# TensorE fetches 36 chunks in place of 32, in turns of 20 late chunks and six fetched ones, with two pairs of tiles in every fifth slot

## The chip, the cores and the metric

One core of one Trainium2 chip runs the whole kernel. The metric is the device time of one execution in microseconds. The kernel before takes 2099.15 us, the median of three runs (2098.36 to 2101.49).

## The reference, cut to what matters

A graph has 6250 nodes with 64 features each and 200,000 edges, sorted by destination. Five graph layers are mixed. All of them are sums over the edges that end in a node, of features of the edge's source:

```python
seg = lambda v: jax.ops.segment_sum(v, dst, num_segments=n)
xs = x[src]
norm = edge_weights / jnp.sqrt(deg_w[src] * deg_w[dst])
gcn = seg(norm[:, None] * xs) @ Wgcn + bgcn
sage = x @ Wsage_s + seg(xs) / deg_c[:, None] @ Wsage_n + bsage
agg_w = seg(edge_weights[:, None] * xs)
gin = ((1.0 + gin_eps) * x + agg_w) @ Wgin + bgin
gconv = x @ Wgc1 + agg_w @ Wgc2 + bgc
eop = seg(edge_weights[:, None] * relu(xs + edge_attr)) @ Wedge + bedge
out = layernorm(x + einsum('k,knd->nd', weights, stack([gcn, sage, gin, gconv, eop])))
```

The work is in two steps per edge: fetch the row of its source node (`xs`), and add products with it to the row of its destination.

## The kernel before

Edges are cut into 196 chunks of 1024, each of 8 tiles of 128 edges. As the edges are sorted, a chunk's destinations lie in a window of 40 nodes. For a chunk, VectorE builds "hots" (for each edge a row of 40 zeros and one entry: 1, the weight, the weight times the root of the degree), adds the edge's attributes to the fetched features, and ScalarE takes the ReLU. TensorE multiplies the features with the hots, tile by tile, into a PSUM bank (`segment_sums`, L1272), and VectorE adds the 40 columns to the sums in SBUF (`add_sums`, L1076). The node rows are fetched in one of three ways:

- *Early* chunks (EARLY = 16): GpSimd gathers raw rows of x before the degrees are known.
- *Late* chunks (148): GpSimd issues eight indirect DMAs per chunk (L572) from a table in DRAM into a ring of UNROLL = 4 chunks. It may write a place of the ring again when TensorE's product of the chunk four before is done (`chunk_product`).
- *Fetched* or *picked* chunks (PICKED = 32): TensorE does the fetch. A chunk is two *units* of HALF = 4 tiles; a unit is two *pairs* of tiles. The node number of an edge is split into a key (node // 7, one of up to 128 partitions where the table lies) and a digit. SP loads the chunk's keys to all partitions (`load_keys`). ScalarE turns them into one-hot matrices for a pair, seven Squares (L696) and one Relu (L699), into one half of `node_hot` (`hot_nodes`). TensorE multiplies each tile's seven one-hots with the high and the low part of the node table in SBUF, 14 matmuls of 462 columns (`pick_tile`, L1293), into one of two PSUM banks. VectorE masks out the digit (L999) and sums (L1003) (`pick`), and after the second pair of a unit does the unit's hots and features (`unit_features`). ScalarE takes the unit's ReLU (`relu_unit`, L687), TensorE its product, 8 matmuls (`unit_product`), VectorE adds it (`add_unit`).

A loop of 4 early steps does the 16 early chunks with the first 16 late ones. Then 16 turns (ROUNDS) follow, the first written out, the other 15 a loop on each of TensorE, ScalarE, VectorE and SP. A turn has 8 *slots* m: each does one late chunk and one pair, so that four slots make one fetched chunk and a turn two. The four last late chunks are the plain step (PLAIN = 1). After that come the output products. GpSimd's gathers are written out for all late chunks. The order on every engine is written by hand as these loops give it, and semaphores with counts hold them together; an engine does nothing ahead of its order.

On TensorE a slot is: late product, two tiles of picks, and in every second slot the product of a unit. On ScalarE: one-hots of the pair, ReLU of the late chunk, and in every second slot the ReLU of a unit. On VectorE: features of the late chunk (waits for its gathers), add of the chunk four before, weights on the hots, then the picks of the pair that TensorE did in the slot before. On SP every second slot issues the attributes of two late chunks (512 KB), each followed by the attributes of a half chunk (128 KB), and once per fetched chunk the keys (256 KB).

The functions that the diff touches, as they are before:

## Time and profile before

| | |
|---|---|
| median of three runs | 2099.15 us |
| profiled execution | 2085.72 us, span 2083.9 us |
| granted TensorE clock, mean | 0.858 |
| TensorE matmul / weight load | 1441.4 us (69%) / 1266.5 us (61%) |
| VectorE / ScalarE / GpSimd | 51% / 44% / 61% |
| late gathers | 1184, 1146.5 us busy |
| matmuls of picks | 3584, 1445.5 us, overlapping |
| DMA | 125.65 MB, mean 60 GB/s |

The profile is one execution. PE is TensorE's matmuls, PEld its weight loads, which run beside them, DVE VectorE, ACT ScalarE, POOL GpSimd, SP the queue that issues most DMAs. A matmul's shown length overlaps with the next one's, so the distance from start to start is what it costs. A group's row has its line, engine, operation, tiles, shapes and count, then the busy time and mean of one, then the idle time of the engine before it and who ended it; "issue" is idle time that nobody's work ended, "remote" a release that the profile can't name. Clock 1.00 is 2.4 GHz.

### The profile page before, as it was taken

To read this page: it belongs to the slowest core of one execution; us is meant where nothing else is said; L and a number is where in the kernel's file an instruction comes from. 1 tells how busy PE (TensorE), PEld (TensorE's weight loads), DVE (VectorE), ACT (ScalarE), POOL (GpSimd) and SP (SyncE) were. 2 spreads that over 40 slices of the span, in tenths; PEclk is the share of its full clock that TensorE was granted. 3 is DMA by queue.
4 is the path that set the end of the run, shared out by engine and by line. 5 is a ranking of instruction groups with operands and counts; after the bars stand their busy time and mean duration, and the time that the engine had idled before them with its cause. 6 is when DMAs were issued, how large, how long until landed. Compare 5 with 4: busy or idle time off the path is not lost.

```text
span 2083.9 us, 26839 instructions
## 1 busy us (share of the span) xinstructions
PE 1441.4 (69%) x7381; PEld 1266.5 (61%) x7381; DVE 1053.7 (51%) x2851; ACT 907.1 (44%) x1515; POOL 1273.2 (61%) x1330
## 2 busy tenths in 40 slices
PE   2000565566877777787877877778788788877876
PEld 1000565565766666676766766667667667756766
DVE  6846274663544445544544544444544454444447
ACT  3847132324544444444544544444544444434433
POOL 6664646665666666666666666666666665666660
PEclk9999986767888888888988888878988988888978
DMA  5111143322222222222222222222222222222214
GB/s 100 24 24 29 43 129 99 103 83 69 53 55 55 53 53 54 61 64 54 54 53 67 53 54 54 54 53 53 56 65 59 54 54 52 67 55 53 55 45 95
DMA packets 86857, 125.65 MB, mean 60 GB/s; under 512 B 28796, under 2 KB 38763, under 8 KB 85463
## 3 DMA queue, kind: packets, MB, share of 16 engines
q0 software_dynamic: 41984, 45.50, 12.8%
q1 hardware_dynamic: 43109, 78.08, 11.8%
q10 hardware_dynamic: 1650, 1.04, 0.3%
q14 instruction: 101, 0.83, 0.1%
q8 instruction: 13, 0.21, 0.0%
HBM read 121.09 MB, written 3.42 MB: 60 GB/s over the span
## 4 chain that ended last, share of the span: by engine, by line
PE 36%; another core or an unknown queue 20%; issue 20%; DVE 11%; ACT 10%; DVEq 2%; DMA 0%; ACTq 0%
PE psum L1293 22%; PE psum L1272 11%; ACT ring L614 4%; ACT node_hot L696 3%; DVE early L1003 2%; DVE ring L1087 2%; DVE sums L1076 2%; PE psum L1325 1%; DVE early L999 1%; ACT ring L662 1%; DVE early L1020 1%; PE psum L1354 1%; PE psum L1355 1%; DVEq L1076 0%
## 5 line engine op out<-in xcount | busy, mean ns | idle before, releaser
L572 POOL DMA_INDIRECT ring<-node_table,e_src x1184 | 1146.5, 968 | 694.7 <-issue 327.2
L1293 PE MATMUL psum<-table_hi,node_hot 128*128 128x462 f32 x1792 | 730.8, 408 | 71.0 <-issue 44.6
L1293 PE MATMUL psum<-table_lo,node_hot 128*128 128x462 f32 x1792 | 714.8, 399 | 40.2 <-issue 39.7
L1272 PE MATMUL psum<-ring 128*128 128x120 f32 x2368 | 371.6, 301 | 228.3 <-issue 180.0
L999 DVE TENSOR_TENSOR early<-psum,digit_hot 128x455 f32<-128x455 f32 x256 | 157.9, 629 | 696.4 <-remote 518.6
L1272 PEld LDWEIGHTS psum<-ring 128*128 128x128 f32 x2368 | 331.7, 212 | 259.5 <-issue 239.3
L696 ACT ACTIVATE node_hot<-early,minus_ids 128x256 fp32r<-128x256 f16 x896 | 370.6, 494 | 239.2 <-remote 205.6
L1293 PEld LDWEIGHTS psum<-table_hi,node_hot 128*128 128x128 f32 x1792 | 370.3, 207 | 146.8 <-issue 71.8
L1293 PEld LDWEIGHTS psum<-table_lo,node_hot 128*128 128x128 f32 x1792 | 369.7, 206 | 97.0 <-issue 55.5
L687 ACT ACTIVATE early<-early 128x256 f32<-128x256 f32 x64 | 26.8, 418 | 600.3 <-DVE early L1020 462.7
L699 ACT ACTIVATE node_hot<-node_hot,ones 128x1792 fp32r<-128x1792 f32 x128 | 229.5, 1793 | 4.2
L1272 PE MATMUL psum<-early 128*128 128x120 f32 x768 | 125.6, 320 | 65.2 <-ACT early L682 46.5
L1076 DVE TENSOR_TENSOR sums<-sums,psum 64x40 f32 (+1 forms) x684 | 134.9, 197 | 56.6 <-remote 21.3
L1272 PEld LDWEIGHTS psum<-early 128*128 128x128 f32 x768 | 120.6, 233 | 70.1 <-ACT early L682 53.7
L538 POOL DMA_INDIRECT early_x<-in_x,early_idx x128 | 122.0, 953 | 65.1 <-issue 47.9
L1003 DVE TENSOR_REDUCE early<-early 128x65 f32<-128x455 f32 x256 | 147.4, 618 | 0.0
L1087 DVE TENSOR_TENSOR ring<-ring,psum 128x320 f32<-128x320 f32 x296 | 131.1, 484 | 4.6
L662 ACT ACTIVATE ring<-attr 128x512 f32<-128x512 f32 x148 | 91.3, 617 | 87.7 <-issue 45.0
L881 DVE SCALAR_TENSOR_TENSOR early<-attr,scratch,psum 128x1024 bf16<-128x1024 f32 x80 | 98.6, 1276 | 37.4 <-issue 37.0
L614 ACT ACTIVATE ring<-attr,scratch 128x1024 bf16<-128x1024 f32 x82 | 93.3, 1138 | 35.0 <-issue 34.1
L1247 PE MATMUL psum<-ring 128*128 128x98 f32 (+1 forms) x8 | 2.0, 435 | 153.1 <-DVE ring L898 153.1
L964 DVE TENSOR_TENSOR attr<-attr,ring 128x512 f32<-128x512 f32 x148 | 101.4, 685 | 0.0
(160 smaller groups left out, 748.2 us busy)
## 6 DMA issues: line engine op xcount, KB each, us to landing
attr<-in_edge_attr SPq DMA_DIRECT2D x73, 512.0 KB
ring<-node_table,e_src POOLq DMA_INDIRECT x1184
src_all<-in_src SPq DMA_DIRECT2D x8, 1024.0 KB
early<-key_rows SPq DMA_DIRECT2D x32, 256.0 KB
early<-in_edge_attr SPq DMA_DIRECT2D x64, 128.0 KB
early<-in_edge_attr SPq DMA_DIRECT2D x16, 256.0 KB
early_x<-degree_rows SPq DMA_DIRECT2D x2, 1568.0 KB, 14.7
early_x<-in_x,early_idx POOLq DMA_INDIRECT x128
```

Source lines behind the costliest of these rows:

```text
L538: nc.gpsimd.indirect_dma_start(out=early_x[:, c, j], out_offset=None, in_=x, in_offset=bass.IndirectOffsetOnAxis(ap=early_idx[:, c, j:j + ...
L572: nc.gpsimd.indirect_dma_start(out=feat[:, u, j, D:BLOCK], out_offset=None, in_=table, in_offset=bass.IndirectOffsetOnAxis(ap=e_src[:, c + ...
L614: last = nc.scalar.activation(signs[0:rows, k % TURNS], row_dst[0:rows, g], ACT.Sign, bias=cuts[0:rows, n:n + 1], scale=-1.0, accum_out=si ...
L662: nc.scalar.activation(feat[:, u, :, 0:D], attr[:, u], ACT.Relu).then_inc(relu_ready, 1)
L696: last = nc.scalar.activation(to[:, :, a], keys_of[k][:, tile:tile + 2], ACT.Square, bias=minus_ids[:, a:a + 1])
L699: nc.scalar.activation(to, to.bitcast(F32), ACT.Relu, bias=ones[:, 0:1], scale=-2.0).then_inc(node_hot_made, 1)
L999: nc.vector.tensor_tensor(out=picks[:, k % 2], in0=pick_ps[k % 2].rearrange("p (b c) -> p c b", b=SPLIT)[:, 0:D + 1], in1=hot_c, op=ALU.mu ...
L1003: last = nc.vector.tensor_reduce(out=feat_g[:, half, k, D:2 * D + 1], in_=picks[:, k % 2], axis=AX.X, op=ALU.add)
L1076: last = nc.vector.tensor_tensor(out=sums[of, k, to], in0=sums[of, k, to], in1=acc[ps, part * WINDOW:(part + 1) * WINDOW], op=ALU.add)
L1087: return nc.vector.tensor_tensor(out=to[:, :, k], in0=to[:, :, 0], in1=by.unsqueeze(2).to_broadcast([P, n, WINDOW]), op=ALU.mult)
L1272: last = nc.tensor.matmul(to[:, 0:3 * WINDOW], features[:, j, 0:2 * D], hots[:, j].rearrange("p k n -> p (k n)"), start=(j == 0), stop=(j ...
L1293: last = nc.tensor.matmul(pick_ps[k % 2], node_hot[:, k, a], part[:, a * SPLIT:(a + 1) * SPLIT].rearrange("p b c -> p (b c)"), start=a == ...
```

## The change

PICKED goes from 32 to 36, so 144 chunks are late. A turn has SLOTS = 20 slots and TURN_CHUNKS = 6 fetched chunks, 24 pairs; there are 6 turns, of which the first is written out, and PLAIN = 2 steps of four chunks at the end. `slot_of` puts pair g into a slot: slots 4, 9, 14 and 19 get two pairs, the others one. `TAKEN` has VectorE take each pair one place later in the order than it is made; `FEATURED` says in which slot a unit's features and ReLU come; the unit's product on TensorE is in the slot after it, now ahead of the slot's picks. Keys stay in two buffers (KEYS = 2).

```diff
-PICKED = 32
+PICKED = 36
-SLOTS = 4
+SLOTS = 20
-TURN_CHUNKS = 2
-TURN_STEPS = TURN_CHUNKS * SLOTS // UNROLL
+TURN_CHUNKS = 6
+TURN_STEPS = SLOTS // UNROLL
+TURN_UNITS = 2 * TURN_CHUNKS
+PAIRS = 2 * TURN_UNITS
+KEYS = 2
-PLAIN = 1
+PLAIN = 2
...
+        def slot_of(g):
+            return g // 6 * 5 + min(g % 6, 4)
+        FETCHED = [[g for g in range(PAIRS) if slot_of(g) == m] for m in range(SLOTS)]
+        TAKEN = [[(g - 1) % PAIRS for g in FETCHED[m][:1]] + FETCHED[m][:-1] for m in range(SLOTS)]
+        FEATURED = {u: slot_of(2 * u + 1) + 1 for u in range(-2, TURN_UNITS)}
+        def unit_at(m, later=0):
+            return next((u for u in FEATURED if FEATURED[u] + later == m), None)
+        def units_added(m):
+            return sum(FEATURED[u] + 1 < m for u in FEATURED) - 2
...
@@ SP, turn
+                    for m in range(SLOTS):
                         if m % 2:
                             load_attributes(EARLY_STEPS + s * TURN_STEPS + m // UNROLL, m % UNROLL // 2)
+                        for k in range(TURN_CHUNKS):
+                            if m == slot_of(4 * k - 5) + 5:
+                                load_keys(s * TURN_CHUNKS + k, k, begun or k >= KEYS)
+                        for u in range(-2, TURN_UNITS - 2):
+                            if m == FEATURED[u] + 5:
+                                load_unit(s * TURN_CHUNKS + (u + 2) // 2, u % 2)
+                        if m in (0, 2) and begun:
+                            load_unit(s * TURN_CHUNKS - 1, m // 2)
...
@@ ScalarE, turn
-                        hot_nodes(s, 2 * c + r // 2, m // SLOTS, r // 2, r % 2)
-                        late_chunk(EARLY_STEPS + s * TURN_STEPS + m // UNROLL, m % UNROLL)
+                        for g in FETCHED[m]:
+                            hot_nodes(s, s * TURN_UNITS + g // 2, g // 4, g // 2 % 2, g % 2)
+                            if g == FETCHED[m][0]:
+                                late_chunk(EARLY_STEPS + s * TURN_STEPS + m // UNROLL, m % UNROLL)
+                        u = unit_at(m)
+                        if u is not None and (begun or u >= 0):
+                            relu_unit(s * TURN_UNITS + u, u % 2)
...
@@ VectorE, turn: features, add and weigh_hots of the late chunk stay
-                        if r in (1, 3) and (begun or m > SLOTS):
-                            dve.wait_ge(added_g, v * UNITS + 2 * c + (r == 3))
+                        elif (begun or m > 2) and (m == 0 or units_added(m) != units_added(m - 1)):
+                            dve.wait_ge(added_g, v * UNITS + s * TURN_UNITS + units_added(m) + 1)
+                        for g in TAKEN[m]:
+                            if m == 0:
+                                if begun:
+                                    take(s * TURN_UNITS - 1, s * TURN_CHUNKS - 1, g)
+                            else:
+                                take(s * TURN_UNITS + g // 2, s * TURN_CHUNKS + g // 4, g)
+                        n = unit_at(m, 1)
+                        if n is not None and (begun or n >= 0):
+                            add_unit(s * TURN_UNITS + n, s * TURN_CHUNKS + n // 2, i * UNROLL + u - LAG + 1)
+                def take(n, c, g):
+                    half, pair = g // 2 % 2, g % 2
+                    pick(n, c, half, (2 * pair, 2 * pair + 1))
+                    if pair:
+                        unit_features(n, c, half)
...
@@ TensorE, turn
-                        late_chunk(i, u)
-                        for pair in range(2):
-                            pick_tile(2 * c + r // 2, 2 * (r % 2) + pair)
-                        if r == 3:
-                            unit_product(2 * c, 0)
-                        if r == 1 and (begun or m > SLOTS):
-                            unit_product(2 * c - 1, 1)
+                        late_chunk(EARLY_STEPS + s * TURN_STEPS + m // UNROLL, m % UNROLL)
+                        u = unit_at(m, 1)
+                        if u is not None and (begun or u >= 0):
+                            unit_product(s * TURN_UNITS + u, u % 2)
+                        for g in FETCHED[m]:
+                            for k in range(2):
+                                pick_tile(s * TURN_UNITS + g // 2, 2 * (g % 2) + k)
```

## Rows read from the trace of the kernel before

**Rows 1.** The page's first part: busy time, share of the span, instructions, by engine
```profile
PE 1441.4 (69%) x7381; PEld 1266.5 (61%) x7381; DVE 1053.7 (51%) x2851; ACT 907.1 (44%) x1515; POOL 1273.2 (61%) x1330
```

**Rows 2.** One line's instructions, L662: 484 to 2027 us, and 499.5 to 656.9 us
```profile
L662 ACT ACTIVATE ring<-attr x129: 609/613/637, 484.1 to 2026.4; 128x512 f32<-128x512 f32 x129
...
L662 ACT ACTIVATE ring<-attr x14: 610/612/616, 499.7 to 656.5; 128x512 f32<-128x512 f32 x14
```

**Rows 3.** Busy time by stretch, turns and end: busy us (instructions) by engine, clock, DMA
```profile
core 0: us, PE busy (x) PEld busy (x) DVE busy (x) ACT busy (x) POOL busy (x), PEclk, DMA share, GB/s
484.00:2026.00 1542.00, 1220.58 (x6106) 1057.52 (x6107) 731.42 (x2114) 681.73 (x1208) 981.09 (x1018) 0.85 0.24 56
2026.00:2084.00 58.00, 40.78 (x299) 39.15 (x298) 41.26 (x94) 20.69 (x26) 5.80 (x7) 0.88 0.38 88
```

**Rows 4.** Timelines of GpSimd and ScalarE from 1990 us on: start, length, instruction
```profile
2023.94 0.94 POOL L572 DMA_INDIRECT ring<-node_table,e_src  x1 [3.33 <-remote]
...
2032.69 0.94 POOL L572 DMA_INDIRECT ring<-node_table,e_src  x1 [0.30 <-issue]
...
2010.29 0.61 ACT L662 ACTIVATE ring<-attr 128x512 f32<-128x512 f32 x1
...
2047.74 0.63 ACT L662 ACTIVATE ring<-attr 128x512 f32<-128x512 f32 x1 [5.80 <-DVE attr L964]
```

**Rows 5.** Groups of instructions by line, GpSimd, 484 to 2026 us
```profile
L572 POOL DMA_INDIRECT ring<-node_table,e_src x1018 | 981.2, 964 | 567.0 <-issue 281.5 <-remote 190.6 <-PE psum L1272 94.9
```

**Rows 6.** Timeline of TensorE, a slot in a clear stretch
```profile
528.98 1.05 PE L1272 MATMUL psum<-early 128*128 128x120 f32 x8
529.86 1.95 PE L1272 MATMUL psum<-ring 128*128 128x120 f32 x16
531.58 0.46 PE L1293 MATMUL psum<-table_hi,node_hot 128*128 128x462 f32 x1
...
537.57 0.93 PE L1272 MATMUL psum<-ring 128*128 128x120 f32 x7
```

**Rows 7.** Busy time by stretch: first and last stall, and a clear stretch
```profile
512.80:524.00 11.20, 6.17 (x12) 3.06 (x13) 0.63 (x1) 0.00 (x0) 6.60 (x7) 0.68 0.25 67
2011.60:2023.70 12.10, 3.70 (x14) 2.86 (x13) 0.68 (x2) 0.00 (x0) 6.87 (x8) 0.65 0.27 66
888.00:910.00 22.00, 21.63 (x132) 19.83 (x130) 12.14 (x34) 10.74 (x19) 15.19 (x16) 1.00 0.23 57
```

**Rows 8.** Timeline of TensorE, a stall and the matmuls after it
```profile
1008.29 0.37 PE L1293 MATMUL psum<-table_hi,node_hot 128*128 128x462 f32 x1
...
1012.86 0.55 PE L1293 MATMUL psum<-table_hi,node_hot 128*128 128x462 f32 x1 [0.19 <-issue]
1015.00 0.55 PE L1293 MATMUL psum<-table_lo,node_hot 128*128 128x462 f32 x1 [1.59 <-issue]
1016.38 0.55 PE L1293 MATMUL psum<-table_hi,node_hot 128*128 128x462 f32 x1 [0.84 <-issue]
...
1019.92 0.59 PE L1293 MATMUL psum<-table_lo,node_hot 128*128 128x462 f32 x1
1020.30 0.59 PE L1293 MATMUL psum<-table_hi,node_hot 128*128 128x462 f32 x1
```

**Rows 9.** Who waited for whom on TensorE, 484 to 2026, then 275 to 450 us
```profile
PE psum L1272 <- issue: 177.9, 198, 3.4
...
PE psum L1293 <- issue: 84.3, 113, 2.6
...
PE psum L1272 <- ACT ring L662: 39.7, 22, 10.0
...
PE psum L1293 <- DVE early L999: 25.2, 15, 3.4
...
PE psum L1272 <- issue: 10.6, 4, 3.2
```

**Rows 10.** DMA queues, 430 to 650 us, then 650 to 2040 us
```profile
q8 instruction: 8, 0.13, 0.2%
...
q14 instruction: 80, 0.66, 0.1%
```

More of the change, by code:

```diff
@@ L216, in build @@
         key_all = key_all.bitcast(F16)
-        keys_of = [key_all[:, k * CHUNK:(k + 1) * CHUNK].rearrange("p (j e) -> p j e", e=P) for k in range(TURN_CHUNKS)]
+        keys_of = [key_all[:, k * CHUNK:(k + 1) * CHUNK].rearrange("p (j e) -> p j e", e=P) for k in range(KEYS)]
         picks = picks.rearrange("p (s c b) -> p s c b", s=2, b=SPLIT)[:, :, 0:D + 1]
@@ L317, in build @@
         key_ready, key_stored = sem("key_ready"), sem("key_stored")
-        key_loaded = [sem(f"key_loaded{k}") for k in range(TURN_CHUNKS)]
+        key_loaded = [sem(f"key_loaded{k}") for k in range(KEYS)]
         key_bias_set, key_row_step = sem("key_bias_set"), sem("key_row_step")
@@ L473, in turn @@
                 def turn(s, begun=True):
-                    for m in range(TURN_CHUNKS * SLOTS):
-                        k, r = m // SLOTS, m % SLOTS
-                        c = s * TURN_CHUNKS + k
+                    for m in range(SLOTS):
                         if m % 2:
                             load_attributes(EARLY_STEPS + s * TURN_STEPS + m // UNROLL, m % UNROLL // 2)
-                        if r == 1:
-                            if begun or k:
-                                load_unit(c - 1, 1)
-                            else:
-                                sp.wait_ge(early_product, (v + 1) * EARLY + 1)
-                            load_keys(c, k, begun)
-                        if r == 3:
-                            load_unit(c, 0)
+                        if m == 1 and not begun:
+                            sp.wait_ge(early_product, (v + 1) * EARLY + 1)
+                        for k in range(TURN_CHUNKS):
[6 more added lines that the diff above has]
+                            load_unit(s * TURN_CHUNKS - 1, m // 2)
                 turn(0, begun=False)
@@ L701, in turn @@
                 def turn(s, begun=True):
-                    for m in range(TURN_CHUNKS * SLOTS):
-                        c, r = s * TURN_CHUNKS + m // SLOTS, m % SLOTS
-                        hot_nodes(s, 2 * c + r // 2, m // SLOTS, r // 2, r % 2)
-                        late_chunk(EARLY_STEPS + s * TURN_STEPS + m // UNROLL, m % UNROLL)
-                        if r == 0 and (begun or m):
-                            relu_unit(2 * c - 1, 1)
-                        if r == 2:
-                            relu_unit(2 * c, 0)
+                    for m in range(SLOTS):
+                        for g in FETCHED[m]:
[5 more added lines that the diff above has]
+                            relu_unit(s * TURN_UNITS + u, u % 2)
                 far_sources(0, 0, 0)
@@ L1032, in turn @@
                 def turn(s, begun=True):
-                    for m in range(TURN_CHUNKS * SLOTS):
+                    for m in range(SLOTS):
                         i, u = EARLY_STEPS + s * TURN_STEPS + m // UNROLL, m % UNROLL
-                        c, r = s * TURN_CHUNKS + m // SLOTS, m % SLOTS
                         if u == 0:
@@ L1046, in turn @@
                             add_early(EARLY - 1, EARLY - LAG + 1)
-                        if r:
-                            half, pair = (r - 1) // 2, (r - 1) % 2
-                            pick(2 * c + half, c, half, (2 * pair, 2 * pair + 1))
-                            if r == 2:
-                                unit_features(2 * c, c, 0)
-                        elif begun or m:
-                            pick(2 * c - 1, c - 1, 1, (2, 3))
-                            unit_features(2 * c - 1, c - 1, 1)
-                            add_unit(2 * c - 2, c - 1, i * UNROLL + u - LAG + 1)
-                        if r == 2 and (begun or m > SLOTS):
-                            add_unit(2 * c - 1, c - 1, i * UNROLL + u - LAG + 1)
+                        for g in TAKEN[m]:
[12 more added lines that the diff above has]
+                        unit_features(n, c, half)
                 def add(c, turn, first):
@@ L1134, in _ @@
                         features(i, u, last=i == LATE_STEPS - 1)
-                        if slot in (1, 3):
-                            dve.wait_ge(added_g, v * UNITS + UNITS + (slot == 3))
+                        if slot < 3:
+                            dve.wait_ge(added_g, v * UNITS + UNITS + slot - 1)
                         add(i * UNROLL + u - LAG, u - LAG, firsts[u])
@@ L1142, in _ @@
                             add_unit(UNITS - 2, PICKED - 1, i * UNROLL + u - LAG + 1)
-                        if slot == 2:
+                        if slot == 1:
                             add_unit(UNITS - 1, PICKED - 1, i * UNROLL + u - LAG + 1)
@@ L1343, in _ @@
                         late_chunk(i, u)
[L1344 to L1345 removed]
+                        if i == LATE_STEPS - PLAIN and u < 2:
+                            unit_product(UNITS - 2 + u, u)
             for g in range(GROUPS):
```

32 lines of the change are left out of this document (15 added, 17 removed).

## The prediction

> **What bounds the kernel now.** I read the page's first part, then the starts of one repeated instruction, busy time by stretch, what GpSimd does at the end, TensorE's timeline in a clear slot and in a bad one, and its waits.
>
> The page's shares give no bound: TensorE 69%, GpSimd 61%, nobody full [rows 1]. The stretch that the change touches has 128 slots, each with one late chunk and one pair of picked tiles. The ReLU of a late chunk (L662) marks a slot: the first of the stretch starts at 484.1 us, the one 128 later at 2026.4 [rows 2], so 1542.3 us, or 12.05 us a slot. That is 74% of the span, and in it TensorE is busy 1220.6 of 1542 us at a mean clock of 0.85, GpSimd 981.1 [rows 3].
>
> Two engines could set 12.05 us. GpSimd issues eight gathers per late chunk; seven steps from 2023.94 to 2032.69 make 1.25 us for each [rows 4], so 10.0 us a slot, and it waits the other 2.05: 190.6 + 94.9 us over the stretch for others [rows 5]. TensorE in a slot at full clock: the 16 matmuls of the late chunk take 1.72 us (529.86 to 531.58), the 28 of two picked tiles 5.99 (531.58 to 537.57, 0.21 each), the 8 of a half unit, due every second slot, 0.88 [rows 6]. Sum: 1.72 + 5.99 + 0.44 = 8.15 us. Over 128 slots that is 1043 us; the other 499 us, 3.90 a slot, TensorE does not work, or works at less than full clock. Most of it is one pattern. In some 34 places of the stretch TensorE all but stops for about 12 us: 12 and 14 matmuls in the first and the last of them, where a clear stretch does 132 in 22 us [rows 7]. Within one, neighbours of the same accumulation start 2.1 and 1.4 us apart with no other engine to release them ("issue"), and after it a matmul of the same shape takes 0.59 us in place of 0.37 and starts every 0.38 in place of 0.21, which is the 1.2 and no more the 2.4 GHz level [rows 8]. Of waits for other engines TensorE shows little: 39.7 us for the ReLU, 25.2 for VectorE's pick (L999), against 177.9 and 84.3 of "issue" [rows 9]. So 65 of the 499 us are waits that other work could fill, and 434 are stalls and slow clock. TensorE bounds the slot, and GpSimd is second with 2 us of slack.
>
> By the Trainium skill (Perfetto Trace Analysis, Identifying the Most-Contended Engine) matmul busy time is no measure for TensorE, and weight-load busy time is to be read: here 1057.5 of 1542 us, 69% [rows 3]. That would leave room on TensorE and is the case of rival C; the releasers of its gaps speak against it.
>
> **The change part by part.**
> (1) Late chunks go from 148 to 144. The 16 of the early stage stay, so 128 + 4 become 120 slots + 8 plain chunks.
> (2) A slot now carries 1.2 pairs (24 in 20) and 0.6 half units (12 in 20): 1.72 + 1.2 x 5.99 + 0.6 x 0.88 = 9.44 us at full clock, +1.29. GpSimd's 10.0 us a slot stands. ScalarE is busy 681.7 us of the 1542, 5.3 a slot, VectorE 731.4, 5.7 a slot [rows 3]; with 1.2 times that each stays below 7 us and hides behind TensorE's 9.4. That cover is gone only if TensorE's slot fell below 7.
> (3) The 3.90 us of lost time. If the stalls come per slot, per late chunk or per microsecond, they stay. The waits in it (65 / 128 = 0.5 a slot) can be filled by the added picks: lower end 3.4. I take 3.7, nearer the upper end, since the chain pick, features, ReLU, next one-hots still runs once per half unit. Slot: 9.44 + 3.7 = 13.14 (12.8 to 13.35). 120 of them: 1577 us (1541 to 1602). Against 1542: +35 (0 to +60).
> (4) The plain end. Before, from the last slot's ReLU at 2010.3 to the last at 2047.7, 37 us pass with four plain chunks [rows 4]. There now are eight, TensorE has no picks there, and the gathers go on at 10.0 us a chunk: +40 if GpSimd has no lead. The ring holds four chunks, and with more slack GpSimd fills it: part of the 40 is prepaid. Lower end +20, I take +32.
> (5) Loop ends. Six rounds of 20 slots in place of 16 of 8, ten fewer on every engine. TensorE's waits name none, so 0; if each had cost its longest "issue" gap, 3.4 us [rows 9], -34.
> (6) The size of TensorE's loop: 8 slots are 8 x 32 + 8 x 56 + 4 x 16 = 768 weight loads and matmuls, 20 slots 640 + 24 x 56 + 12 x 16 = 2176. Queue 8 moves 8 instruction packets, 0.13 MB or 16 KB each, from 430 to 650 us, and has no row from 650 to 2040 [rows 10]: I read it as TensorE's code, resident from then on. While it moved, slots were no slower: 13 of them from 499.7 to 656.5 us, 12.06 each [rows 2]. So fetching ahead costs 0; a jump back to code that has gone costs between 0 and one stall of 12 us [rows 7], at five loop ends: 0 to +60. I take +6, nearest to the 0 of straight code.
> The Trainium skill (Runtime: NRT & Kernel Launch, Instruction fetch mechanics) has TensorE's instruction memory at 2048 instructions in blocks of 256, and a taken branch out of it must fetch first. By that rule the new loop no longer fits, and the sum would be at the upper end of (6); the trace agrees with the block size, and shows no such branch.
> (7) Before the loops, 36 in place of 32 keys and digits: under 1 us. Four more key loads and eight more half-unit loads on SP's queue replace two of the attribute loads. SP issues in order behind waits for ReLUs, two slots ahead as before. VectorE's wait for added_g moves by a slot; behind it are queued its own adds and picks, for which TensorE waits, but what it waits for is its own add of an earlier slot: 0.
> (8) Two pairs in every fifth slot. The second pair's one-hots use the other half of the buffer and cost ScalarE some 4.5 us (5.3 less the ReLUs) against TensorE's 5.99, so 0. If the order added a wait, one 3.4 us gap in each of 24 such slots, +82; I take 0.
>
> Sum: +35 + 32 + 6 = +73 us. On the profiled execution (2085.7 us around a span of 2083.9) that is 2159. The median of the runs is 2099.15, 13 above it; on it **2172 us**.
>
> **Rivals.**
> *B, stalls follow the picks.* From 275 to 450 us, with no picks, TensorE's "issue" before L1272 is 10.6 us in all [rows 9], and afterwards there are 34 stalls for 32 picked chunks. If the picks make them, they cost 434 x 36/32 = 488 us in place of 434 x 120/128 = 407: +81 on the forecast, 2253. Against: in the trace they keep no fixed place in a turn.
> *C, GpSimd's pace decides, and the added picks fall into time that TensorE loses now.* Then a late chunk costs 12.05 us as today, and four fewer save 48: 2051 us. Place: the slot; price: -12.05 per chunk removed; it brings a gain as long as a slot stays below (1542 - 32) / 120 = 12.6 us, for which the lost time has to fall from 3.90 to under 3.1. For it: GpSimd's waits are many and short (190.6 us, [rows 5]), and longer runs of matmuls keep the clock up. Against: filling every wait for others reaches only 3.4.
> *D, the stalls belong to the turn.* Two per round: 12 in place of 32, each worth 434 / 34 = 12.8 us: 256 less, 2172 - 256 = 1916; GpSimd's 1200 us for 120 slots allow it. Against: the first, unrolled turn has them as well (512.8 us, [rows 7]).
> *E, the loop thrashes.* Each of nine blocks in five rounds stalls TensorE by 12 us less the 2 of work in it: +450, 2622. Against: see (6).
>
> **How the numbers follow.** Forecast 0.43, B 0.19, C 0.20, D 0.07, E 0.04, and 0.07 for effects that cancel to within 20 us of the old time, of which 0.02 faster, 0.03 the same, 0.02 slower. About 0.2%, 4 us, is what a measurement of this kernel can tell from no change. Faster: 0.20 + 0.07 + 0.02 = 0.29; same 0.03; slower 0.68. The forecast's own range, by the ends of (3) to (6), is 2099 + 20 - 34 = 2085 to 2099 + 160 = 2259; with the 82 of (8) on top it would be 2341, which I leave out. The range takes in C and B and leaves out D and E: 2045 to 2262.
>
> **What would show it.** (2) and (3): the first and the last slot's L662, 120 apart, 1541 to 1602 us from each other, and GpSimd waiting 3 us a slot. B: more than 36 stretches of 12 us with a dozen matmuls; D: a dozen; C: a slot below 12.6 us. (4): 57 to 77 us between the last slot's ReLU and the last one. (6): a row for queue 8 through the whole stretch, and a gap on TensorE every 20 slots. The forecast is wrong if a slot stays below 12.6 us.

## The result, and the profile after

The changed kernel takes **2125.14 us** (median of four, 2121.18 to 2129.47), the one before, run beside it, 2098.86 (2098.36 to 2101.49): ratio **1.0121**, 95% interval 1.0097 to 1.0145. In a later session (after_again, chip 6) it was 1.0053 (1.0022 to 1.0084). The change makes the kernel slower, by 26 us and not by the 73 that I forecast. The profiled execution went from 2085.7 to 2121.2 us, its span from 2083.9 to 2119.4.

The page's first part (busy time, share, instructions) answers to [rows 1]:
```profile
PE 1499.5 (71%) x7829; PEld 1332.6 (63%) x7829; DVE 1090.4 (51%) x2954; ACT 984.1 (46%) x1647; POOL 1242.1 (59%) x1298
```
L684 is the late chunk's ReLU now. The first row below lists its starts from the first slot to the first plain chunk, 120 later, the second those up to the last; they answer to [rows 2, 4]:
```profile
L684 ACT ACTIVATE ring<-attr x121: 607/613/636, 487.7 to 2028.2; 128x512 f32<-128x512 f32 x121
...
L684 ACT ACTIVATE ring<-attr x128: 607/613/636, 487.7 to 2080.0; 128x512 f32<-128x512 f32 x128
```
With them the 35.5 us of the span split without remainder:

| stretch | before | after | difference | forecast |
|---|---|---|---|---|
| start to the first slot's ReLU | 484.1 | 487.7 | +3.6 | 0 |
| slots, to the first plain ReLU | 1542.3 (128) | 1540.5 (120) | -1.8 | +35, loops +6 |
| first plain ReLU to the last | 21.3 (4 chunks) | 51.8 (8) | +30.5 | +32 |
| last ReLU to the end | 36.2 | 39.4 | +3.2 | 0 |

All of the miss is in the second line: a slot takes 12.84 us, where the forecast had 13.14. TensorE's work in it is 9.44 us at full clock, so 3.40 are lost, against 3.90 before. The 120 slots' 1540.5 us lie just under the 1541 to 1602 that were to show the forecast true. The last of the 120 intervals alone took 27.0 us (before 16.1); without it a slot is 12.72 us.

Busy time of the slots and of the end (columns as in [rows 3]), GpSimd's group (as [rows 5]), TensorE's waits (as [rows 9]; L1298 is the late chunk or half unit, L1319 the pick), and the queues from 650 us on (as [rows 10]):
```profile
487.00:2028.00 1541.00, 1260.54 (x6498) 1105.94 (x6499) 758.45 (x2184) 757.88 (x1336) 922.48 (x960) 0.90 0.23 55
2028.00:2119.00 91.00, 56.44 (x355) 54.19 (x354) 51.33 (x127) 23.27 (x30) 30.81 (x32) 0.76 0.34 78
```
```profile
L594 POOL DMA_INDIRECT ring<-node_table,e_src x960 | 922.5, 961 | 629.0 <-issue 261.3 <-PE psum L1298 194.7 <-remote 173.0
```
```profile
PE psum L1298 <- issue: 143.7, 117, 5.4
...
PE psum L1298 <- ACT ring L684: 66.9, 34, 20.4
PE psum L1319 <- issue: 40.8, 58, 6.9
...
PE psum L1298 <- DVE ring L1113: 24.6, 12, 4.0
...
PE psum L1319 <- DVE early L1021: 13.6, 14, 1.9
```
```profile
q8 instruction: 56, 0.92, 0.3%
q14 instruction: 56, 0.46, 0.1%
```
The reader is to see two movements. TensorE's "issue" time fell from 262.2 to 184.5 us, and the waits for others that these rows show rose from 64.9 to 105.1. Counted in the trace, the stalls of 12 us in the slots went from 34 (414 us) to 16 (205 us), and other pauses of over 0.6 us from 50 (72 us) to 98 (177 us). A stall is a dense run of such pauses, 8 us long or more. With the line drawn a little differently before still has 34 and the kernel after 16 to 19, and in its later session the same kernel had 24: part of the fall to 16 is chance. GpSimd's waits for TensorE and "remote" grew from 285.5 to 367.7 us.

What the stalls hang on shows when GpSimd's timeline is laid beside TensorE's. First GpSimd, kernel after, from 1404 us (the lines left out are gathers 1.25 us apart with 0.30 of "issue"), then TensorE, then that window and a clear one by busy time:
```profile
1409.62 0.95 POOL L594 DMA_INDIRECT ring<-node_table,e_src  x1 [2.69 <-remote]
...
1418.38 0.95 POOL L594 DMA_INDIRECT ring<-node_table,e_src  x1 [0.30 <-issue]
1419.63 0.95 POOL L594 DMA_INDIRECT ring<-node_table,e_src  x1 [0.31 <-issue]
...
1428.39 0.95 POOL L594 DMA_INDIRECT ring<-node_table,e_src  x1 [0.30 <-issue]
1434.52 0.95 POOL L594 DMA_INDIRECT ring<-node_table,e_src  x1 [5.18 <-PE psum L1298]
```
```profile
1418.86 0.38 PE L1319 MATMUL psum<-table_lo,node_hot 128*128 128x462 f32 x1
1421.95 0.93 PE L1298 MATMUL psum<-ring 128*128 128x120 f32 x6 [2.71 <-ACT ring L684]
1423.21 0.26 PE L1298 MATMUL psum<-ring 128*128 128x120 f32 x1 [0.33 <-issue]
1425.31 0.36 PE L1298 MATMUL psum<-ring 128*128 128x120 f32 x1 [1.84 <-issue]
1428.11 0.36 PE L1298 MATMUL psum<-ring 128*128 128x120 f32 x1 [2.44 <-issue]
1430.21 0.36 PE L1298 MATMUL psum<-ring 128*128 128x120 f32 x1 [1.74 <-issue]
1431.61 0.36 PE L1298 MATMUL psum<-ring 128*128 128x120 f32 x1 [1.04 <-issue]
1432.32 1.41 PE L1298 MATMUL psum<-ring 128*128 128x120 f32 x5 [0.35 <-issue]
```
```profile
1418.90:1432.30 13.40, 2.96 (x13) 2.01 (x11) 2.89 (x10) 0.63 (x1) 8.00 (x9) 0.67 0.15 25
1440.00:1462.00 22.00, 21.16 (x122) 18.98 (x122) 13.47 (x38) 12.92 (x25) 11.33 (x12) 1.00 0.23 57
```
Eight gathers are one chunk. At 1409.62 GpSimd begins a chunk after a pause, at 1419.63 the next one with none. From that moment matmuls of one accumulation start 1.4 to 2.8 us apart, until 3 us after the sixteenth gather ends. Going back to the kernel before with this in hand: 34 of 128 chunks there begin less than 1.5 us after the end of the gather before them ("no pause" from here on), and the 34 stalls begin each within -1.0 to +2.7 us of one of these. The stall of [rows 8] is one; GpSimd in the kernel before:
```profile
996.47 0.94 POOL L572 DMA_INDIRECT ring<-node_table,e_src  x1 [2.56 <-remote]
...
1006.67 0.94 POOL L572 DMA_INDIRECT ring<-node_table,e_src  x1 [0.31 <-issue]
...
1020.13 0.94 POOL L572 DMA_INDIRECT ring<-node_table,e_src  x1 [3.79 <-remote]
```
In the kernel after there are 19 such chunks and 16 stalls, all at one of them. What lets GpSimd go on is an early product of TensorE, the one that frees its place in the ring. Laid side by side in the trace of before (124 chunks): where it was done 5 us or more ahead of the end of the last gather, 28 of 41 chunks began with no pause, at 3 to 5 us 5 of 19, and later than that none of 64. I had read GpSimd by its sum and its waits, and never against the stalls.

### The profile page after: what moved, and what is told of

It is laid out like the page before. It is cut to its first block, busy times and chain, and to the rows that moved or that the text cites. A ratio compares the mean times of both kernels' runs of the same rounds, so it can differ in the third digit from the quotient of the medians.

```text
span 2119.4 us, 27847 instructions
## 1 busy us (share of the span) xinstructions
PE 1499.5 (71%) x7829; PEld 1332.6 (63%) x7829; DVE 1090.4 (51%) x2954; ACT 984.1 (46%) x1647; POOL 1242.1 (59%) x1298
## 4 chain that ended last, share of the span: by engine, by line
PE 36%; issue 27%; another core or an unknown queue 17%; DVE 9%; ACT 7%; DVEq 2%; SPq 1%; POOL 1%; DMA 0%; ACTq 0%; POOLq 0%
PE psum L1319 21%; PE psum L1298 12%; ACT node_hot L718 5%; PE psum L1349 1%; DVE early L1021 1%; DVE sums L1102 1%; DVE early L1025 1%; DVE ring L1113 1%; ACT ring L684 1%; DVE attr L986 1%; POOL ring L594 1%; PE psum L1378 1%; PE psum L1379 1%; DVEq L1102 0%
## 5 line engine op out<-in xcount | busy, mean ns | idle before, releaser
L594 POOL DMA_INDIRECT ring<-node_table,e_src x1152 | 1115.0, 968 | 770.2 <-issue 314.9
L1319 PE MATMUL psum<-table_hi,node_hot 128*128 128x462 f32 x2016 | 788.8, 391 | 39.7 <-issue 24.9
L1319 PE MATMUL psum<-table_lo,node_hot 128*128 128x462 f32 x2016 | 773.3, 384 | 16.5 <-issue 15.8
L718 ACT ACTIVATE node_hot<-early,minus_ids 128x256 fp32r<-128x256 f16 x1008 | 417.4, 495 | 460.1 <-remote 325.0
L1298 PE MATMUL psum<-ring 128*128 128x120 f32 x2304 | 362.5, 312 | 265.0 <-issue 140.8
L1298 PEld LDWEIGHTS psum<-ring 128*128 128x128 f32 x2304 | 334.6, 223 | 301.9 <-issue 230.1
L1021 DVE TENSOR_TENSOR early<-psum,digit_hot 128x455 f32<-128x455 f32 x288 | 177.2, 629 | 591.2 <-remote 422.1
L1319 PEld LDWEIGHTS psum<-table_hi,node_hot 128*128 128x128 f32 x2016 | 396.3, 197 | 106.5 <-issue 39.0
L1319 PEld LDWEIGHTS psum<-table_lo,node_hot 128*128 128x128 f32 x2016 | 395.2, 196 | 69.3 <-issue 24.6
L721 ACT ACTIVATE node_hot<-node_hot,ones 128x1792 fp32r<-128x1792 f32 x144 | 258.2, 1793 | 4.7
L1298 PE MATMUL psum<-early 128*128 128x120 f32 x832 | 140.6, 326 | 62.9 <-issue 29.7
L684 ACT ACTIVATE ring<-attr 128x512 f32<-128x512 f32 x144 | 89.1, 619 | 187.3 <-DVE attr L986 134.4
L1298 PEld LDWEIGHTS psum<-early 128*128 128x128 f32 x832 | 129.7, 238 | 67.1 <-ACT early L704 35.1
L1025 DVE TENSOR_REDUCE early<-early 128x65 f32<-128x455 f32 x288 | 165.9, 619 | 0.0
L636 ACT ACTIVATE ring<-attr,scratch 128x1024 bf16<-128x1024 f32 x82 | 93.3, 1140 | 34.6 <-issue 33.7
```

The costliest lines, as they stand in the source:

```text
L594: nc.gpsimd.indirect_dma_start(out=feat[:, u, j, D:BLOCK], out_offset=None, in_=table, in_offset=bass.IndirectOffsetOnAxis(ap=e_src[:, c + ...
L684: nc.scalar.activation(feat[:, u, :, 0:D], attr[:, u], ACT.Relu).then_inc(relu_ready, 1)
L718: last = nc.scalar.activation(to[:, :, a], keys_of[k % KEYS][:, tile:tile + 2], ACT.Square, bias=minus_ids[:, a:a + 1])
L721: nc.scalar.activation(to, to.bitcast(F32), ACT.Relu, bias=ones[:, 0:1], scale=-2.0).then_inc(node_hot_made, 1)
L1021: nc.vector.tensor_tensor(out=picks[:, k % 2], in0=pick_ps[k % 2].rearrange("p (b c) -> p c b", b=SPLIT)[:, 0:D + 1], in1=hot_c, op=ALU.mu ...
L1025: last = nc.vector.tensor_reduce(out=feat_g[:, half, k, D:2 * D + 1], in_=picks[:, k % 2], axis=AX.X, op=ALU.add)
```

## The experiments

The ratio is to the kernel before in the same session. Slot: ReLU to ReLU as above; "no pause": chunks of the slots that begin under 1.5 us after the last gather; both from the one profiled execution.

| kernel | ratio (95%) | TensorE's work / slot, us | no pause, stalls |
|---|---|---|---|
| before | 1 | 8.15 / 12.05 | 34, 34 |
| after; after_again | 1.0121 (1.0097-1.0145); 1.0053 (1.0022-1.0084) | 9.44 / 12.84; 12.72 | 19, 16; 25, 24 |
| long4; long8 | 1.0002 (0.9982-1.0022); 0.9976 (0.9952-1.0000) | 8.15 / 11.94; 12.00 | 35, 35; 36, 37 |
| order_short | 1.0051 (1.0023-1.0080) | 8.15 / 12.07 | 33, 27 |
| prod_last | 1.0628 (1.0589-1.0666) | 9.44 / 13.74 | 1, 1 |
| old_order | 1.0712 (1.0642-1.0782) | 9.44 / 13.91 | 20, 15 |
| work_down | 0.9935 (0.9915-0.9954) | 6.87 / 11.99 | 40, 39 |
| work_up | 1.0239 (1.0197-1.0281) | 9.43 / 12.45 | 25, 24 |
| order_up | 1.0330 (1.0306-1.0355) | 9.43 / 12.61 | 27, 25 |
| halfway | 0.9995 (0.9971-1.0019) | 8.15 / 12.00 | 32, 32 |
| filler | 1.0033 (1.0010-1.0056) | 8.15 / 12.13 | 35, 35 |
| land; land_again | 0.9782 (0.9752-0.9812); 0.9796 (0.9775-0.9816) | 8.15 / 11.90; 11.92 | 0, 0 |
| land_half | 0.9894 (0.9868-0.9921) | 8.15 / 11.93 | 31, 28 |
| land_up | 0.9868 (0.9844-0.9892) | 9.43 / 11.91 | 0, 0 |
| after_land; after_land_again | 0.9764 (0.9734-0.9795); 0.9728 (0.9705-0.9752) | 9.44 / 12.09; 12.17 | 0, 0 |
| after_land_cut | 0.9658 (0.9630-0.9687) | 9.44 / 12.38 | 3, 1 |

**First: turns, code, order.** Before I had seen GpSimd's part, three theories stood for the halved stalls: T, they belong to the turn; R, to whether the code stays resident; S, to the slot, and the new order in it halves them. long4 and long8 are the kernel before with longer turns:
```
-TURN_CHUNKS = 2
+TURN_CHUNKS = 4        # long8: 8; keys stay in two buffers, k % 2
```


> The kernel before with turns of 16 slots and 4 fetched chunks in place of 8 and 2 (8 turns in place of 16); order inside a slot, the 32 fetched chunks and the 148 late ones as before. Theory T (the 12 us stalls of TensorE belong to the turn, two of them in each, as rival D had it): 16 stalls in place of 34, each worth some 12 us with the slow clock after it, so 150 to 220 us less, unless the freed time turns into waits as in the changed kernel, where 16 stalls remain and the lost time per slot fell only from 3.90 to 3.40 us: then some 40 to 60 us less, 2040 to 2060. Theory R (the stalls follow from code that stays resident and is jumped back to, and go where code streams through): no change here, since 16 slots of code are about 1536 matmuls and weight loads and stay under the size at which queue 8 began to move: 34 stalls, 2099. Theory S (stalls come per slot or per microsecond, and the new order in the slot halved them): 34 stalls, 2099.

> The kernel before with turns of 32 slots and 8 fetched chunks (4 turns), all else as before. TensorE's loop is some 3072 matmuls and weight loads, so queue 8 moves throughout. Theory T: 8 to 10 stalls, 2040 or less. Theory R: about half of the stalls go as in the changed kernel, 15 to 17 remain, 2040 to 2060, while long4 stays at 2099. Theory S: 34 stalls, 2099.

Stalls and slot did not move (35 and 37 stalls), though queue 8 moved 67 and 56 packets between 484 and 2010 us, against 6 in before. T and R fall. It also shows that TensorE's code came through queue 8 at 16 slots a turn already: my count in (6) had the size too generous. Streamed straight on it costs nothing that shows. A jump back does cost something: at the six jumps of long4 TensorE's matmuls pause for 1.0 to 3.1 us with nobody to wait for, in before at 14 jumps for 0.1 to 0.7. (6) took +6 us for its jumps, which is of that size.

order_short has the new order alone (PICKED 32, eight slots, one pair each, one plain step), prod_last the kernel after with the unit's product behind the picks:
```
                         late_chunk(...)
-                        (unit_product, if one is due)
                         for g in FETCHED[m]: picks
+                        (unit_product, if one is due)
```


> The changed kernel's order (a unit's product ahead of the slot's picks, its add in the same slot and no longer one after) at the old ratio and turn: 8 slots, one pair each, 2 fetched chunks, 32 in all. Theory S: the stalls fall to about 16 as in the changed kernel, 2040 to 2060. Theories T and R: 34 stalls; the time within 10 us of 2099, since the order alone moves 0.88 us of products ahead of 5.99 us of picks.

> The changed kernel with the unit's product put back behind the picks of its slot. Theory S: stalls rise from 16 towards 34 and the time by 20 to 60 us above 2125. Theories T and R: 16 stalls; VectorE's add of the unit, which waits for the product, comes up to 12 us later in slots with two pairs, and the gathers and picks behind it: 0 to 40 us above 2125 from that alone.

order_short has fewer stalls (27) and more pauses for others (72, 168 us, against 50 and 72 us) at the same slot: the order swaps one loss for another. The traces show where: VectorE sits idle at each jump back of its own loop, 2.6 to 4.1 us with, but for one case, nobody to wait for, in all ten kernels that I read for it. In the old order TensorE hardly feels it; in the new one its matmuls pause there as well. VectorE's first instruction of a turn and TensorE's late product, order_short, the first jump back:
```profile
664.97 0.49 DVE L1104 TENSOR_TENSOR ring<-e_win,psum 128x320 f32<-128x320 f32 x1 [3.60 <-issue]
...
668.16 2.07 PE L1294 MATMUL psum<-ring 128*128 128x120 f32 x8 [7.52 <-DVE ring L1110]
```
TensorE's pauses at the 15 turn boundaries sum to 66 us in order_short and to 3 in before. In the kernel after, with five, they sum to 14: ten fewer turns saved TensorE nothing, since they had cost it nothing.

prod_last has one stall, 370 us of other pauses and 13.74 us a slot: stalls vanish as TensorE waits more, and the sum is not better for it. At 1.0628 it is some 106 us above after, where 0 to 60 were expected. The stall was a response, to something that a waiting TensorE doesn't set off. That sent me to GpSimd's timeline, and to theory G: TensorE all but stops while GpSimd issues a chunk's gathers with no pause after those of the chunk before.

**Second: the pauses of GpSimd.** In land it waits, before each chunk, for the landing of the chunk before:
```
                     pool.wait_ge(chunk_product, v * LATE + c + 1)
+                    if c:
+                        pool.wait_ge(gathered[(c - 1) % UNROLL], (v * LATE_STEPS + (c - 1) // UNROLL) * (16 * TILES) + 16 * TILES)
                     pool.sem_inc(gathers_begun, 1)
```


> The kernel before, in which GpSimd waits, ahead of each late chunk's eight gathers, until those of the chunk before have landed. In the trace of before, all 29 runs of 16 gathers without a pause have a TensorE stall in their second half, and 71 runs of 8 have five. Theory G (the gathers make the stalls: TensorE all but stops while GpSimd issues a second chunk's gathers with no pause after the first): no stalls of 12 us are left (at most 3), GpSimd's chunk is 10.0 us and a pause of 2.3 to 3.8, and paces the slot at 12.3 to 13.8 us: 2082 + 32 to 2082 + 220, I take 12.8 a slot, 2180. Theory S (the stalls belong to TensorE's own running, and GpSimd's unbroken runs only follow from them): about 30 stalls stay, and the slot is over 13 us, since the pauses come on top.

No stall is left and the kernel is 2.2% faster, 2054.54 us. GpSimd's timeline in land, then its group and TensorE's wait, 484 to 1950 us:
```profile
1001.90 0.95 POOL L574 DMA_INDIRECT ring<-node_table,e_src  x1 [2.17 <-issue]
...
1013.89 0.98 POOL L574 DMA_INDIRECT ring<-node_table,e_src  x1 [2.28 <-issue]
...
1025.94 0.95 POOL L574 DMA_INDIRECT ring<-node_table,e_src  x1 [2.31 <-issue]
...
1037.94 1.00 POOL L574 DMA_INDIRECT ring<-node_table,e_src  x1 [2.29 <-issue]
```
```profile
L574 POOL DMA_INDIRECT ring<-node_table,e_src x976 | 926.7, 950 | 537.3 <-issue 503.2 <-DMA ring<-node_table,e_src 34.1
```
```profile
PE psum L1274 <- DVE ring L1089: 335.4, 122, 4.2
```
A chunk every 12.0 us, like clockwork, and a TensorE that waits 335 us, 2.75 a time. Adding a wait of 2.3 us per chunk to the engine that I had called second brought the time down. G had the stalls right and the time wrong (12.8 us a slot and 2180 us expected, 11.90 and 2054.54 measured): the wait took the place of the 2.05 us a slot that GpSimd had waited anyway. By stretch the span's 25.8 us are: before the slots -33.7, slots -18.6, first plain ReLU to the last +22.2, rest +4.3. So the larger gain lies ahead of the slots. There the kernel before issues its first 32 gathers in one go (213.2 to 256.6 us), and TensorE, still making the node products, stops, and ScalarE with it:
```profile
237.97 0.42 PE L1234 MATMUL psum<-ident,sums 128*64 128x128 f32 x1
255.80 1.97 PE L1239 MATMUL psum<-W_node,early 65*128 65x64 f32 x8 [17.41 <-issue]
```
```profile
246.76 0.37 ACT L646 COPY parts_h<-psum 128x256 f32<-128x256 f32 x1 [10.61 <-issue]
```
ScalarE's copy starts 8.6 us after the product that it reads is done (238.18); the copies before it start within 0.2 us of theirs. In land, with a pause after each eight, the first ReLU of the edge loop starts at 250 us, in before at 274. The early stretch of [rows 9] began at 275 us and missed this. Theory G stands; S, by which the stalls are TensorE's own, falls.

work_up and work_down change TensorE's work in the kernel before by 1.28 us a slot and nothing else:
```
+                    for _ in range(3):
+                        nc.tensor.matmul(pick_ps[k % 2], node_hot[:, k, 0],
+                                         table_hi[:, 0:SPLIT].rearrange("p b c -> p (b c)"), start=True, stop=True)
                     for a in range(SPLIT):
                         for part in (table_hi, table_lo):
+                            if part is table_lo and a in (3, 4, 5):   # work_down, in place of the three above
+                                continue
```


> The kernel before, with three more matmuls for each picked tile (the first one again, which starts its bank anew, so nothing computed changes): 6 x 0.214 = 1.28 us more of TensorE's work per slot, what the change adds, and nothing else of it. As the prediction has it (step 3: lost time stays 3.7 to 3.9 a slot): +1.28 x 128 = +164 us, 2246, about 34 stalls. Theory G: TensorE's slot without a stall grows from 9.7 to 11.0 us, over GpSimd's 10.0, its product comes later and GpSimd pauses more often: 10 to 18 stalls, a slot of 12.3 to 12.8, +30 to +96 us, I take 2140.

> The kernel before without three of the 14 matmuls of each picked tile (the low parts of three of seven blocks are left out, so fetched rows keep only their high parts there): 1.28 us less of TensorE's work per slot. Additive: -164 us, 1918. Theory G: TensorE gets ahead of GpSimd more often, and more runs of 16 gathers stall it: 38 to 50 stalls, slot 11.7 to 12.1, 0 to -45 us, I take 2060.

1.28 us more cost 0.40 (24 stalls left, more than the 18 that I allowed G), 1.28 less gave 0.06 (39 stalls). This is the change's own step (3), isolated: TensorE's work is not additive here.

> The kernel after, with the order in a slot of the kernel before: the half unit's product behind the slot's picks, and its sums added one slot later. Order theory (the new order is what brought the stalls down from 34 to 16): about 30 stalls again, slot 13.1, after + 25 to + 40 us, 2150. Theory G with the ratio as the cause (more TensorE work a slot leaves GpSimd its pauses): 10 to 20 stalls, slot 12.8 to 12.9, within 10 us of after, 2125 less the 17 us by which this chip's before was faster, if it is the same chip.

Its edit beside prod_last's: `unit_at(m, 2)` for the sums. 15 stalls, as G wants, but 13.91 us a slot and 298 us of other pauses: with 0.6 units a slot the product behind the picks is late. Both expectations missed its time; the change's new order is needed at its ratio.

**Third: what of the pause matters.** halfway has land's wait ahead of the fifth gather (`if c and j == 4`), filler three one-column memsets ahead of the first and no wait.

> The kernel before, with the same wait for the landing of the chunk before, but ahead of a chunk's fifth gather, not of its first: GpSimd may go from chunk to chunk with no pause, but its sequencer can't run ahead by a whole chunk. If the stall comes from gathers issued with no pause: runs of 16 stay and stall TensorE, 30 to 40 stalls, ratio 0.99 to 1.01. If it comes from a sequencer that has run ahead and sits before a later wait: no runs with stalls, GpSimd's slot is 10.0 to 10.6 us, TensorE's 8.15 plus clock and waits sets 10.5 to 11.3, ratio 0.87 to 0.94. If each such wait costs a restart of its own (2.3 us): GpSimd paces 12.3 to 14.6, ratio 1.0 to 1.15.

> The kernel before, with three small memsets on GpSimd ahead of each chunk's gathers and no wait added: some 0.3 to 0.9 us in which it issues no gather, with no change in what its sequencer may run ahead of. If a short pause between gathers is enough to keep TensorE going: stalls fall under 10 and the slot to 11 to 11.7, ratio 0.93 to 0.98. If only a pause by a wait does it: 25 to 35 stalls stay, ratio 1.0 to 1.03.

> The kernel before with the landing wait ahead of every second late chunk (the odd ones) only. Theory G by dose: GpSimd can pass without a pause only ahead of an even chunk, at most once in two slots; no run is longer than 16 gathers, all stalls begin at an even chunk, and there are 25 to 50 of them, ratio 0.99 to 1.01. If the landing wait helped in some other way (spreading of the transfers), half of it would bring half of the gain: 15 to 20 stalls, ratio 0.985 to 0.99.

halfway keeps 32 chunks with no pause and 32 stalls. Its wait held nothing up (10 gaps of over 1.6 us ahead of a fifth gather, 9 in before): it shows that a wait in the code that is met when it is reached changes nothing, and that a sequencer free to run ahead is not the cause. What a real pause inside a chunk would do isn't tested. filler did not test what it was built for. Where GpSimd may go on, the memsets fill the usual gap and no pause arises:
```profile
1046.73 0.95 POOL L575 DMA_INDIRECT ring<-node_table,e_src  x1 [0.30 <-issue]
1047.68 0.18 POOL L573 MEMSET filler<- 128x1 bf16 x3
1048.00 0.94 POOL L575 DMA_INDIRECT ring<-node_table,e_src  x1
```
and a stall follows (13 matmuls from 1048.1 to 1061.1). Whether a pause without a wait would do stays open. How long it has to be can be read from all 20 traces together, though in none was it set on purpose. In the slots 31 chunks began 0.4 to 1.1 us after the end of the last gather, and TensorE started 5 to 23 matmuls from 1 to 12 us behind their beginning, much as after no pause at all (median 11). Over 1.75 us the median is above 50. So 1 us is too little, and 2 us mostly enough.

land_half leaves 31 chunks with no pause, all at even chunks, and 28 stalls, five of them not at such a chunk (this count, too, moves by a few with the line drawn); they are shorter (10.1 us). The stalls are as G by dose has them, but the ratio, 0.9894, is what the rival (spreading of the transfers) expected. The traces say why: 25 of the 29 us come ahead of the slots, where the 32 gathers in one go are broken up too; a slot takes 11.93 us against 12.05. The stall is bound to the missing pause, but its length isn't fixed at 12 us.

**Fourth: the change with the stalls gone.** after_again and after_land ran in one session (before: 2082.98 us), land_again, after_land_again and after_land_cut in a later one (before: 2097.66 us); both were on chip 6. after_land_cut drops the wait ahead of the last eight chunks (`if 0 < c < LATE - 8`).

> The kernel after, unchanged, on this chip beside the others: ratio 1.008 to 1.016, 12 to 20 stalls, slot 12.8 to 12.9 us; it is what after_land is read against.

> The kernel after, with GpSimd's wait for the landing of the chunk before (as in land). In land GpSimd needs 11.90 us a late chunk, and TensorE waits some 3 us a slot for it. Theory G with GpSimd as the bound: the change's 1.29 us of TensorE's work per slot fits in those 3 us, the slot stays 11.9 to 12.1, no stalls, and four late chunks fewer save 4 x 11.9 = 48 us against land: 0.978 - 0.023 = 0.955 of before (0.95 to 0.965). Rival W (the added work costs its own time whatever GpSimd does): slot 13.2, 120 x 1.3 - 48 = +108 against land, 1.03 of before. Between them: double slots wait for the order of picks and sums, slot 12.3 to 12.6, 0.98.

> The kernel before with the landing wait, unchanged, on one chip beside after_land_again: ratio 0.974 to 0.982 of before, no stalls, slot 11.8 to 12.0 us.

> The kernel after with the landing wait, on the same chip. If the change is worth its four late chunks once the stalls are gone (GpSimd's bound): 15 to 30 us under land_again, ratio 0.962 to 0.970. If the added work and the longer plain end take it back: within 6 us of it, ratio 0.974 to 0.980.

> after_land without the landing wait ahead of the last eight late chunks, where TensorE has no picks. If GpSimd's pace alone (10.0 with, 12.3 us without leave to go on) sets the plain end: 10 to 18 us under after_land_again. If runs of gathers with no pause stall TensorE there as well (16 matmuls of a late chunk at 0.7 us are 11 us): 0 to +15 us.

> land with the three more matmuls a tile of work_up: 1.28 us more of TensorE's work per slot, and GpSimd paced by the landings. With land alone the slot is 11.9 us and TensorE waits some 3 us of it. If the work falls into those waits: slot 11.9 to 12.2, 0.98 to 0.99 of before, no stalls. If it comes on top: slot 13.2, 1.06 of before.

land_up settles the disputed term: with the pauses kept, 1.28 us more of TensorE's work per slot costs 0.01 us (11.91 against 11.90), or 0.14 at most. The first row is its ReLU's starts, 128 slots; the second its busy time from 484 to 1968 us; the third TensorE's wait, 335.4 in land:
```profile
L664 ACT ACTIVATE ring<-attr x129: 609/630/633, 443.5 to 1968.2; 128x512 f32<-128x512 f32 x129
```
```profile
484.00:1968.00 1484.00, 1291.45 (x6697) 1159.88 (x6695) 711.88 (x2070) 668.86 (x1169) 938.33 (x989) 0.93 0.24 56
```
```profile
PE psum L1274 <- DVE ring L1089: 190.0, 119, 3.0
```
Its median, 2054.76 us, is that of land (2054.54), though on a chip where before took 2084.85 and not 2100.67, so that the ratio is 0.9868. The two were not run side by side; if the ratios are what counts, the 1.28 us cost 18 us, 0.14 a slot. TensorE carries 9.43 of 11.91 us here, 79%. By the Trainium skill (Perfetto Trace Analysis, Identifying the Most-Contended Engine) weight-load busy time, not matmul busy time, tells how full TensorE is. The 69% of [rows 3] did leave room, and land_up went to 78% (1159.88 of 1484) at next to no cost: that rule was right, and I set it aside.

With the wait, the change is a gain: 2039.65 after 2055.16 us, -15.5, of the 15 to 30 expected. Slots fall from 128 x 11.92 to 120 x 12.17 (-65), and from the first plain ReLU to the last it takes 92.7 us, not 43.9 (+49), since GpSimd paces that end at 12 us a chunk. after_land alone, at 0.9764, had missed the 0.95 to 0.965 expected for want of this term. Letting GpSimd go on there gives back 13.4 us. **after_land_cut, 2026.28 us, beats both kernels**: 0.9658 of before.

> order_short (the new order in a slot, at one pair a slot and turns of 8) with the three more matmuls a tile of work_up: TensorE's average work per slot is the one of after, with no double slots and no long turn. work_up had 12.45 us a slot, after 12.84 and 12.70. If the new order is what costs after the rest: 12.7 to 12.9, ratio 1.035 to 1.05. If the double slots (or the long turn) do: 12.4 to 12.55, ratio 1.02 to 1.03.

order_up came between its two expectations, at 12.61. Over work_up's 12.45, the new order costs 0.16 (by the ratios 0.15). That can't be carried over to after as it stands: order_up has 15 turn boundaries, at which TensorE pauses 64 us in all (work_up 10), and after has five with 14 us. The 0.27 to 0.39 us that after has over work_up are with the order, its turn boundaries (14 us over 120 slots, 0.12 a slot), the double slots or the work of ScalarE and VectorE, and these weren't told apart; two executions of after differ by 0.12 themselves.

## Why the prediction was right or wrong

Right: the sign; the plain end, +32 forecast as the price of four more chunks and +30.5 measured from the first plain ReLU on, though by (4)'s own mark, from the last slot's ReLU to the last, it went from 37.4 to 78.8 us, +41 and over the 57 to 77 given (67 in the later session, +30); GpSimd's waits, 3 us a slot (367.7 / 120 = 3.06); the streaming of code, nearly free; loop ends worth 0 in the kernel before, (5), though the new order then made TensorE pause at them. (7) and (8), taken at nothing, may have some part in the 0.27 to 0.39 us a slot that after lies above work_up.

**The step that failed is (3), the 3.90 us of lost time, taken as 3.7.** I split it by what ended each gap: 434 us of "issue" and slow clock that no other work could fill, 65 us of waits that it could. From that came the floor of 3.4, and 13.14 us a slot, +35 us. Measured: 3.40, right on the floor that I had called the lower end, 12.84 a slot and -1.8 us. The split itself was wrong, not only the value: most of the 434 us (34 stalls, 414 us) are what GpSimd does to TensorE when it starts a chunk with no pause, and it gets to do so when TensorE's product is early. More work makes TensorE later, the unbroken starts fall (34, 25 in work_up, 19 and 25 in the two traces of after), and part of the added work is taken from the stalls:

| TensorE's work a slot, us | 6.87 | 8.15 | 9.43 | 9.43, pauses kept |
|---|---|---|---|---|
| lost time, us | 5.12 | 3.90 | 3.02 | 2.48 |

The forecast's constant would be a flat row. The kernel after lies at 3.40 and 3.28 in its two traces, above work_up's 3.02.

*Rival C* named half of the mechanism that holds: "the added picks fall into time that TensorE loses now". Its price asked for lost time under 3.1, and the change reached 3.40, so that 39% of the added 1.29 us was absorbed (12.84 against 13.34) and 61% paid. With the pauses kept it is true in full. Against it I had held that filling every wait reaches only 3.4, which is the same faulty split.
*Rival B* (stalls follow the picks) falls: 36 picked chunks, 16 stalls. *Rival D* (the turn) had a dozen stalls, 16 and 24 were counted, and long4 and long8 tell against it. *Rival E* falls: queue 8 moved 0.92 MB from 650 us on, TensorE's pauses at the five turn boundaries were 0.2, 3.8, 4.4, 2.0 and 3.7 us, the last four put down to VectorE, and long4's slot with its code on the move was no longer than that of before (11.94 against 12.05). By the Trainium skill (Runtime: NRT & Kernel Launch, Instruction fetch mechanics) crossing a block is mostly hidden and only a taken branch out of the window must fetch; packets of 16 KB through the whole stretch at no cost agree with the first, and long4's pauses of 1.0 to 3.1 us at its six jumps back, against 0.1 to 0.7 in before, agree with the second.

So, why slower at all: eight slots fewer take out 96 us, the other 120 pay 0.79 us each for 1.2 pairs, 95 in all, and the four more plain chunks cost 30.5; with the 6.8 us ahead and behind that is the +35.5.

## What to carry to other kernels

Lay the timelines of two engines side by side at a stall before splitting it by its releaser: "issue" says only that the profile names nobody, not that the engine itself is the cause. Lost time is not a constant to add to work; vary the suspected bound's work by a known amount both ways, and the slope (0.31 up, 0.05 down here) tells whether it is the bound at all. When gathers run ahead on GpSimd, try holding them back: one wait per chunk was worth more than the change under study. Look at each engine's own jump back as well: the order of work decides whether another engine feels it.

## What the runs showed of the hardware

Indirect gathers leave GpSimd every 1.25 us, and a chunk that starts on the heels of another slows TensorE from about one matmul per 0.2 us to one per 0.7 to 2 until some 3 us after the last of the sixteen: 34 of 34 times in the kernel before, 35 of 35 in filler, 24 of 25 in work_up, 16 of 19 in after (18 with a looser line). GpSimd can pause although the product that it asks for is there: in the kernel before, of the 33 chunks whose product was done 0 to 3 us ahead of the end of the last gather, all started 1.9 to 3.9 us after that end, half of them within 2.5, and so did some with more lead (done at 989.99, last gather over at 993.91, next at 996.47).

Why unbroken gathers do this to TensorE isn't settled. It is not TensorE's alone, since ScalarE's copy at 246.76 us came 8.6 us late in the same way, the one case of it read here; so something shared is more likely than the delivery of one engine's instructions, but no row names it. The DMA share over the 34 stalls of the kernel before is 0.23 in the mean (0.14 to 0.39), over its other stretches 0.26, so it is not the volume of transfers.

VectorE is idle for 2.6 to 4.1 us at every jump back of its loop; at 13 of the 14 in the kernel before and at all four in after, the idle time is put down to "issue".
